# Prefix steps of a recurrent-block kernel: output projections begun on three channel blocks ahead of the last gate, the other jobs and PSUM banks dealt anew

## The chip, the cores and the metric

One core of a Trainium2 chip. The metric is device time in microseconds. Before the change: 9424.98 us, the median of 3 runs (9423.15 to 9425.7).

## The reference

Two blocks in a row, all in float32. The first is a stack of L = 4 selective state-space layers (width D = 256, inner width DI = 512, DS = 16 states a channel) over a sequence that is a 64-token context prefix followed by 512 tokens, for 16 sequences:

```
p = silu(ctx @ pre_w1) @ pre_w2;  h = concat([p, x], time)
for each layer:
    xn = rmsnorm(h) * norm_w
    xi, z = split(xn @ in_proj)
    xi = silu(causal_conv4(xi) + conv_b)
    dt, Bm, Cm = split(xi @ x_proj);  dt = softplus(dt @ dt_proj + dt_b)
    state[e, s] = exp(dt * A[e, s]) * state[e, s] + dt * Bm[s] * xi[e]      # over time
    y = sum_s state[e, s] * Cm[s] + xi * D_param
    h = h + (y * silu(z)) @ out_proj
h = rmsnorm(h)[:, 64:]
```

The second is a cross-attention and feed-forward block on h and the context.

## The kernel before

**Phases.** Since all is causal, the 64 prefix tokens of all 16 sequences are done first, for all four layers: 8 sequences of 64 tokens side by side fill 512 columns. This gives 8 *prefix steps* (4 layers x 2 halves, class `Phase` with the `PRE_` tables), and their end states are written to HBM (`kept`). Then a loop over 4 blocks of 4 sequences runs 16 *main steps* each (4 layers x 4 sequences, `MAIN_` tables), and the attention part. A step holds one layer of 512 columns.

**A step.** DVE makes 64 scans (line 989), one for each of 4 channel blocks ("chunks" 0 to 3 of 128 channels) and 16 states, in 32 *units* of two. ACT makes the decays (line 727) into a ring of 8, running ahead of the scans; PE makes the scan's inputs with small matmuls (`make_input`, line 442), a *quad* of four scans at a time, into one four-bank PSUM area that isn't doubled. So the input of quad w + 1 waits for the last scan of quad w. POOL multiplies each unit's two states with the C rows (line 1231, `product`), in the prefix after copying the end states to `save` (line 1219, `keep`). PE then adds the products up in the bank `acc` (`sum_pair`, lines 454 and 459), two units behind in the prefix.

**Jobs.** While step n scans, the engines work off *jobs* of three steps: what ends step n - 1, what later chunks of n need, and what prepares n + 1. In the tables, key v is the unit at which an engine takes the job, and the pair (name, rel) says for which step: -1, 0 or 1. Each engine takes its jobs strictly in the table's order, between its own share of the scan work. The names:
- `yev` (ACT, 738) evicts a chunk of y from `acc`; `yt` (PE, 515) transposes it; `gate` (DVE, 1039) multiplies it with silu(z); `out0`, `out1` (PE, 522) are the two halves of the output projection, each four matmul parts, one a chunk; `res` (DVE, 1044) adds the residual.
- `sq` (ACT, 747), `ms` (PE, 478), `rstd` (ACT, 750 to 755) and `norm` (DVE, 999) are the norm; `xi` (PE 484, ACT 776 to 781) and `tap` (DVE, 1017) the convolution; `z` (PE 489, ACT 788) the gate's input; `silu_x`, `silu_z` (ACT, 791 to 803); `xp` (PE 495, ACT 812).
- `bT` turns B; POOL's `diag` (1240) spreads it. `dt` (PE 505, ACT 824 to 829), `ln` (834), `q`, `less`, `ndt` (DVE, 1023 to 1034) are the softplus. `dtx` (POOL, 1252) is dt * xi, `dxT` (PE 510, ACT 839) its transpose, which the inputs of that chunk's quads need; `skip` (ACT, 843) scales xi for the sum.

A name with a point, as out0.2, is one part of it. PE writes a float32 matmul as two records, so a half of the output projection has eight.

**Banks.** Jobs use three PSUM banks, `PRE_BANK` says which. A job waits until what was in its bank before is read (`bank_free`). The pending semaphore waits stand in front of the instruction, so whatever is behind it on that engine waits too. SyncE's queue loads each layer's weights, the C rows and stores the states; its order is fixed by similar waits.

Of the kernel before, what the change touches and what calls it, by code (L numbers as in the profile page):

```python
# [15 lines left out]
KI = DI // P  # L16
# [23 lines left out]
SILU = "silu_and_others"  # L40


PRE_BANK = {"dt0": 2, "dt1": 0, "dt2": 2, "dt3": 0, "dxT0": 1, "dxT1": 1, "dxT2": 2, "yt3": 1, "out0": 0, "out1": 2,
            "dxT3": 1, "ms": 1, "xi0": 0, "xi1": 2, "xi2": 1, "xi3": 0, "yt0": 2, "z0": 2, "z1": 1, "z2": 2, "z3": 0,
            "xp": 1, "yt1": 0, "bT": 1, "yt2": 1}
MAIN_BANK = {"xi0": 2, "xi1": 1, "xi2": 2, "xi3": 0, "z0": 1, "z1": 1, "z2": 1, "z3": 2, "dt3": 2, "yt3": 0, "xp": 1,
             "out0": 0, "bT": 1, "yt0": 2, "dt0": 2, "out1": 1, "dxT3": 0, "dt1": 0, "dxT0": 1, "dt2": 0, "ms": 1,
             "dxT1": 2, "yt1": 1, "yt2": 0, "dxT2": 0}
PARTS = {"ms": KD, "xi": KD, "z": KD, "xp": KI, "out": KI}


PRE_PE = {0: [("dxT1", 0)], 2: [("dxT2", 0)], 3: [("yt3", -1)], 4: [("dxT3", 0), ("out0", -1)], 5: [("out1", -1)],
# [4 lines left out]
PRE_ACT_FIRST = {2: [("yev3", -1)], 10: [("yev0", 0)], 18: [("yev1", 0)], 26: [("yev2", 0)]}  # L57
PRE_ACT = {0: [("ln3", 0)], 1: [("dxT1", 0), ("skip2", 0)], 3: [("dxT2", 0), ("skip3", 0)], 5: [("dxT3", 0)],
# [4 lines left out]
PRE_DVE = {1: [("less3", 0), ("ndt3", 0)], 3: [("gate3", -1)], 5: [("res0", -1)], 7: [("res1", -1)],  # L63
# [6 lines left out]
PRE_POOL = {0: [("dtx2", 0)], 2: [("dtx3", 0)], 28: [("dtx0", 1)], 30: [("dtx1", 1)]}  # L70


MAIN_PE = {0: [("xi3", 1)], 2: [("z0", 1)], 4: [("z1", 1)], 5: [("dt3", 0)], 6: [("z2", 1)], 7: [("yt3", -1)],
# [85 lines left out]
def program(nc, xT, ctxT, w_early, ip_x, ip_z, xp_w, dt_w, op_w, a_log, d_par, pre_w1, pre_w2, cst,  # L159
            cst_attention, avec, wq, wk, wv, wp, w1, w2, b2, kept, c_rows, out):  # L160
    ctx = ExitStack()
    with ctx:
# [69 lines left out]
        sq = view(SLOTS, KD, S)  # L232
# [78 lines left out]
        def await_read_of(eng, ph, m, name):  # L311

            eng.wait_ge(job_read[ph.bank[name]], bank_free(ph, m, name) + 1)  # L313
# [115 lines left out]
        def _(pe):  # L429
# [35 lines left out]
            def job(ph, m, full):  # L465
# [3 lines left out]
                if part:  # L469
                    parts = [parts[int(part[0])]]  # L470
# [3 lines left out]
                if name == "ms":  # L474
                    if 0 in parts:
                        pe.wait_ge(normed.sem, normed.at(ph, m, 1))
                    for k in parts:
                        i = nc.tensor.matmul(o, ones_x, xn[:, k, :], start=k == 0, stop=k == KD - 1)
                elif name[:2] == "xi":
                    if full in ("xi0", "xi0.0"):  # L480
                        pe.wait_ge(ipx_loaded, ph.layers(m) * 16)
                        await_read_of(pe, ph, m, "ms")
                    for k in parts:
                        i = nc.tensor.matmul(o, ipx[:, k, c * P:(c + 1) * P], xn[:, k, :], start=k == 0, stop=k == KD - 1)  # L484
                elif name[0] == "z":
                    if full in ("z0", "z0.0"):
                        pe.wait_ge(ipz_loaded, ph.layers(m) * 16)
                    for k in parts:
                        i = nc.tensor.matmul(o, ipz[:, k, c * P:(c + 1) * P], xn[:, k, :], start=k == 0, stop=k == KD - 1)  # L489
                elif name == "xp":  # L490
                    if 0 in parts:
                        pe.wait_ge(xpw_loaded, ph.layers(m) * 16)
                        pe.wait_ge(silu_x.sem, silu_x.at(ph, m, 1))
                    for k in parts:
                        i = nc.tensor.matmul(o[0:XP, :], xpw[:, k, :], xs[:, par, k, :], start=k == 0, stop=k == KI - 1)  # L495
                elif name == "bT":
                    await_read_of(pe, ph, m, "xp")
                    for b in range(NB):
                        i = nc.tensor.matmul(o[:, b * XP:(b + 1) * XP], xdbl[0:XP, b::NB], eye[0:XP, 0:XP],
                                             start=b == 0, stop=b == NB - 1, is_transpose=True)  # L500
                elif name[:2] == "dt":
                    if c == 0:
                        pe.wait_ge(dtw_loaded, ph.layers(m) * 16)
                        await_read_of(pe, ph, m, "xp")
                    i = nc.tensor.matmul(o, dtw[0:DR + DS + 1, c * P:(c + 1) * P], xdbl[0:DR + DS + 1, :],  # L505
                                         start=True, stop=True)
                elif name[:3] == "dxT":
                    pe.wait_ge(dtx_ready.sem, dtx_ready.at(ph, m, c + 1))
                    for b in range(NB):
                        i = nc.tensor.matmul(o[:, b * P:(b + 1) * P], dtx[:, b::NB], eye, start=b == 0, stop=b == NB - 1,  # L510
                                             is_transpose=True)
                elif name[:2] == "yt":
                    pe.wait_ge(y_out.sem, y_out.at(ph, m, c + 1))
                    for b in range(NB):
                        i = nc.tensor.matmul(o[:, b * P:(b + 1) * P], yT[:, c % 2, b * P:(b + 1) * P], eye,
                                             start=b == 0, stop=b == NB - 1, is_transpose=True)
                else:
                    if full in ("out0", "out0.0"):
                        pe.wait_ge(opw_loaded, ph.layers(m) * 16)
                        await_read_of(pe, ph, m, "yt3")  # L520
                    for k in parts:
                        i = nc.tensor.matmul(o, opw[:, k, c * P:(c + 1) * P], zs[:, m % ZS, k, :],  # L522
                                             start=k == 0, stop=k == KI - 1)
# [943 lines left out]
```

## Time and profile before

| | |
|---|---|
| median of 3 runs | 9424.98 us |
| profiled execution | 9428.24 us, span 9426.4 us |
| PE busy | 7754.2 us (82%) |
| DVE busy | 7468.0 us (79%) |
| POOL busy | 6233.6 us (66%) |
| ACT busy | 5973.5 us (63%) |
| first scan of step 0; of the first main step | 93.2; 1137.2 us |

The prefix steps are those from 93.2 to about 1040 us. Busy shares are over the whole span, of which the prefix is a ninth. The main steps repeat 64 times after it.

### The profile page before, as it was taken

To read this page: it belongs to the slowest core of one execution; us is meant where nothing else is said; L and a number is where in the kernel's file an instruction comes from. 1 tells how busy PE (TensorE), PEld (TensorE's weight loads), DVE (VectorE), ACT (ScalarE), POOL (GpSimd) and SP (SyncE) were. 2 spreads that over 40 slices of the span, in tenths; PEclk is the share of its full clock that TensorE was granted. 3 is DMA by queue.
4 is the path that set the end of the run, shared out by engine and by line. 5 is a ranking of instruction groups with operands and counts; after the bars stand their busy time and mean duration, and the time that the engine had idled before them with its cause. 6 is when DMAs were issued, how large, how long until landed. Compare 5 with 4: busy or idle time off the path is not lost.

```text
span 9426.4 us, 188716 instructions
## 1 busy us (share of the span) xinstructions
PE 7754.2 (82%) x67360; PEld 5217.9 (55%) x67360; DVE 7468.0 (79%) x7794; ACT 5973.5 (63%) x9252; POOL 6233.6 (66%) x3268
## 2 busy tenths in 40 slices
PE   7878688888878788888878788888879788888879
PEld 4555455555563455555553455555554455555554
DVE  5777599999985399999974499999974599999963
ACT  5666477777753477777753577777753577777742
POOL 4777477777771277778761387777761478777751
PEclk8888899999989899999989899999989899999989
DMA  1111111111110111111110111111100111111100
GB/s 58 47 47 42 37 41 46 55 43 43 40 37 16 45 47 54 43 40 43 53 39 3 48 56 40 43 42 56 44 34 5 59 43 40 48 53 43 40 34 10
DMA packets 133365, 390.63 MB, mean 41 GB/s; under 512 B 49580, under 2 KB 78188, under 8 KB 95552
## 3 DMA queue, kind: packets, MB, share of 16 engines
q1 hardware_dynamic: 132416, 378.25, 11.2%
q8 instruction: 562, 9.21, 0.4%
q14 instruction: 387, 3.17, 0.1%
HBM read 364.97 MB, written 13.24 MB: 40 GB/s over the span
## 4 chain that ended last, share of the span: by engine, by line
POOL 47%; issue 32%; PE 7%; POOLq 1%; ACT 1%; DVE 1%; DMA 0%; SPq 0%; DVEq 0%; ACTq 0%
POOL arena L1231 41%; PE ps L545 3%; POOL arena L1252 3%; PE ps L675 2%; POOL arena L1240 2%; POOL arena L1270 1%; POOLq L1227 0%; PE ps L489 0%; PE ps L484 0%; DMA arena<-kept 0%; PE ps L495 0%; PE ps L612 0%; PE ps L672 0%; PE ps L505 0%; POOLq L313 0%
## 5 line engine op out<-in xcount | busy, mean ns | idle before, releaser
L1231 POOL TENSOR_TENSOR arena<-arena 128x1024 f32<-128x1024 f32 x2304 | 5428.9, 2361 | 1489.9 <-DVE arena L989 1451.6
L989 DVE TENSOR_TENSOR_SCAN arena<-arena,ps 128x512 f32<-128x512 f32 x4608 | 5490.4, 1254 | 721.5 <-PE ps L442 531.2
L727 ACT ACTIVATE arena<-arena,rate 128x512 f32<-128x512 f32 (+1 forms) x4608 | 3122.2, 714 | 1104.4 <-DVE arena L989 1098.8
L459 PEld LDWEIGHTS ps<-csts,arena 128*128 128x128 f32 x18432 | 2175.9, 145 | 564.0 <-issue 452.9
L459 PE MATMUL ps<-csts,arena 128*128 128x128 f32 x18432 | 2431.5, 281 | 26.8 <-POOL arena L1231 26.8
L442 PE MATMUL ps<-arena 32*128 32x128 f32 x36864 | 1404.3, 290 | 923.3 <-DVE arena L989 911.7
L442 PEld LDWEIGHTS ps<-arena 32*128 32x128 f32 x36864 | 1176.4, 192 | 1193.2 <-DVE arena L989 1088.3
L484 PE MATMUL ps<-arena 128*128 128x512 f32 x1152 | 681.5, 725 | 253.3 <-DVE arena L999 184.6
L1252 POOL TENSOR_TENSOR arena<-arena 128x512 f32<-128x512 f32 x288 | 365.8, 1270 | 736.7 <-DVE arena L1034 722.9
L489 PE MATMUL ps<-arena 128*128 128x512 f32 x1152 | 601.8, 640 | 18.8 <-DVE arena L1034 12.5
L522 PE MATMUL ps<-arena 128*128 128x512 f32 x1152 | 556.3, 610 | 4.4 <-DVE arena L1039 4.4
L545 PE MATMUL ps<-arena 128*128 128x512 f32 (+2 forms) x1152 | 545.0, 614 | 8.6 <-ACT arena L910 8.6
L484 PEld LDWEIGHTS ps<-arena 128*128 128x128 f32 x1152 | 232.5, 222 | 500.8 <-DVE arena L999 200.8
L1017 DVE SCALAR_TENSOR_TENSOR ps<-arena,ps 128x512 f32<-128x512 f32 x576 | 429.0, 745 | 96.6 <-ACT ps L781 90.7
L1270 POOL TENSOR_TENSOR arena<-arena 128x512 f32<-128x512 f32 x128 | 133.2, 1042 | 537.8 <-DVE arena L1157 537.8
L843 ACT ACTIVATE arena<-arena,Dall 128x512 f32<-128x512 f32 x288 | 206.5, 717 | 293.4 <-POOL arena L1252 293.4
L545 PEld LDWEIGHTS ps<-arena 128*128 128x128 f32 (+1 forms) x1152 | 218.0, 202 | 309.1 <-issue 255.6
L1198 DVE TENSOR_TENSOR arena<-ps,arena 128x256 f32<-128x256 f32 x64 | 27.2, 424 | 418.6 <-PE ps L675 418.6
L505 PE MATMUL ps<-arena 33*128 33x512 f32 x576 | 339.1, 671 | 22.7 <-DVE arena L1034 22.7
L738 ACT ACTIVATE arena<-ps 128x512 f32<-128x512 f32 x288 | 170.1, 590 | 286.2 <-PE ps L459 286.2
L1240 POOL TENSOR_TENSOR arena<-csts,arena 128x512 f32<-128x512 f32 x288 | 300.9, 1046 | 76.3 <-ACT arena L819 76.3
L824 ACT ACTIVATE arena<-ps 128x512 f32<-128x512 f32 x288 | 170.0, 590 | 236.2 <-PE ps L505 236.2
(96 smaller groups left out, 7588.4 us busy)
## 6 DMA issues: line engine op xcount, KB each, us to landing
arena<-c_rows SPq DMA_DIRECT2D x288, 1024.0 KB, 4.6
arena<-ip_x SPq DMA_DIRECT2D x20, 512.0 KB, 3.7
arena<-ip_z SPq DMA_DIRECT2D x20, 512.0 KB, 3.9
arena<-op_w SPq DMA_DIRECT2D x20, 512.0 KB, 3.8
hT<-xT SPq DMA_DIRECT2D x16, 512.0 KB, 5.0
arena<-w SPq DMA_DIRECT2D x8, 1024.0 KB, 8.5
out<-arena SPq DMA_DIRECT2D x64, 128.0 KB, 1.7
arena<-xp_w SPq DMA_DIRECT2D x20, 160.0 KB, 2.4
```

What stands on the lines that cost most here:

```text
L442: i = nc.tensor.matmul(o, dtxT[rows, c, b, :], diagB[rows, quad, b, :].rearrange("p (i s) -> p i s", s=Q), start=True, stop=True)
L459: i = nc.tensor.matmul(acc[:, b * P:(b + 1) * P], hs[:, place(n, v) + s, b * P:(b + 1) * P], eye, start=False, stop=(v + 1) % CU == 0 and ...
L484: i = nc.tensor.matmul(o, ipx[:, k, c * P:(c + 1) * P], xn[:, k, :], start=k == 0, stop=k == KD - 1)
L489: i = nc.tensor.matmul(o, ipz[:, k, c * P:(c + 1) * P], xn[:, k, :], start=k == 0, stop=k == KD - 1)
L522: i = nc.tensor.matmul(o, opw[:, k, c * P:(c + 1) * P], zs[:, m % ZS, k, :], start=k == 0, stop=k == KI - 1)
L545: last = nc.tensor.matmul(o, lhs, rhs, start=i == 0, stop=i == len(parts) - 1)
L727: nc.scalar.activation(o, i, ACT.Exp, scale=rate[:, ph.layer(n), g:g + 1]).then_inc(decay.sem, 1)
L989: nc.vector.tensor_tensor_scan(hs[:, place(n, v) + g % 2, :], dA[:, g % RING, :], quad[:, g % Q::Q], init[:, n % 2, g:g + 1] if ph.main() ...
L1017: i = nc.vector.scalar_tensor_tensor(o, w, taps[:, c, k:k + 1], acc_c, ALU.mult, ALU.add)
L1231: nc.gpsimd.tensor_tensor(hs[:, a:a + 2, :], hs[:, a:a + 2, :], Crep[:, 2 * pair:2 * pair + 2, :], ALU.mult).then_inc(prod.sem, 1)
L1240: nc.gpsimd.tensor_tensor(diagB[:, quad, :, :].rearrange("p b (i s) -> p b i s", s=Q), minus32.unsqueeze(1).unsqueeze(3).broadcast_to(shap ...
L1252: nc.gpsimd.tensor_tensor(dtx, dt[:, c, :], xs[:, m % 2, c, :], ALU.mult).then_inc(dtx_ready.sem, 1)
```

## The change

The four `PRE_` job tables and `PRE_BANK` are rewritten; the `MAIN_` tables stay. The parts out0.0 to out0.2 and out1.0 to out1.2 are put ahead of the last gate of their step, and only out0.3 and out1.3 behind it. For this the code waits for the read of yt2 (its gate) ahead of out0.0, and for that of yt3 ahead of the last part. The norm and what follows are taken earlier, dxT0 to dxT3, dtx and skip are taken later, xp is cut into parts, and all four z use one bank.

```diff
-PRE_BANK = {"dt0": 2, "dt1": 0, "dt2": 2, "dt3": 0, "dxT0": 1, "dxT1": 1, "dxT2": 2, "yt3": 1, "out0": 0, "out1": 2,
-            "dxT3": 1, "ms": 1, "xi0": 0, "xi1": 2, "xi2": 1, "xi3": 0, "yt0": 2, "z0": 2, "z1": 1, "z2": 2, "z3": 0,
-            "xp": 1, "yt1": 0, "bT": 1, "yt2": 1}
+PRE_BANK = {"out0": 1, "out1": 2, "yt3": 0, "dxT1": 0, "ms": 2, "dxT2": 0, "xi0": 1, "xi1": 2, "dxT3": 0, "xi2": 1, "xi3": 2,
+            "z0": 0, "z1": 0, "z2": 0, "z3": 0, "yt0": 1, "xp": 2, "yt1": 1, "bT": 0, "dt0": 2, "dt1": 0, "dt2": 1, "yt2": 2,
+            "dxT0": 2, "dt3": 0}
...
-PRE_PE = {0: [("dxT1", 0)], 2: [("dxT2", 0)], 3: [("yt3", -1)], 4: [("dxT3", 0), ("out0", -1)], 5: [("out1", -1)],
-          8: [("ms", 1)], 12: [("xi0", 1), ("xi1", 1)], 13: [("xi2", 1)], 15: [("xi3", 1)], 16: [("yt0", 0)],
-          18: [("z0", 1), ("z1", 1)], 20: [("z2", 1), ("z3", 1)], 21: [("xp", 1)], 22: [("yt1", 0)],
-          24: [("bT", 1), ("dt0", 1)], 26: [("dt1", 1)], 27: [("yt2", 0)], 28: [("dt2", 1)], 29: [("dxT0", 1)],
-          30: [("dt3", 1)]}
+PRE_PE = {0: [("out0.0", -1), ("out0.1", -1)], 1: [("out0.2", -1)], 2: [("out1.0", -1), ("out1.1", -1)],
+          3: [("yt3", -1), ("out1.2", -1)], 4: [("out0.3", -1), ("out1.3", -1)], 5: [("dxT1", 0)], 7: [("ms", 1)],
+          9: [("dxT2", 0)], 10: [("xi0", 1)], 11: [("xi1", 1)], 13: [("dxT3", 0), ("xi2", 1)], 14: [("xi3", 1)],
+          15: [("z0", 1)], 16: [("z1", 1)], 17: [("yt0", 0), ("z2", 1)], 18: [("z3", 1)], 20: [("xp.0", 1), ("xp.1", 1)],
+          21: [("xp.2", 1), ("xp.3", 1)], 22: [("yt1", 0)], 23: [("bT", 1), ("dt0", 1)], 25: [("dt1", 1)], 27: [("dt2", 1)],
+          28: [("yt2", 0)], 30: [("dxT0", 1), ("dt3", 1)]}
...
-PRE_ACT = {0: [("ln3", 0)], 1: [("dxT1", 0), ("skip2", 0)], 3: [("dxT2", 0), ("skip3", 0)], 5: [("dxT3", 0)],
-           7: [("sq", 1)], 9: [("rstd", 1)], 12: [("xi0", 1)], 13: [("xi1", 1)], 14: [("xi2", 1)], 16: [("xi3", 1)],
-           19: [("z0", 1), ("z1", 1)], 20: [("silu_x", 1), ("z2", 1), ("z3", 1), ("silu_z", 1)], 23: [("xp", 1)],
-           25: [("bT", 1), ("dt0", 1)], 26: [("ln0", 1)], 27: [("dt1", 1)], 28: [("ln1", 1)],
-           29: [("dt2", 1), ("skip0", 1)], 30: [("dxT0", 1), ("ln2", 1)], 31: [("dt3", 1), ("skip1", 1)]}
-PRE_DVE = {1: [("less3", 0), ("ndt3", 0)], 3: [("gate3", -1)], 5: [("res0", -1)], 7: [("res1", -1)],
-           11: [("norm0", 1), ("norm1", 1)], 13: [("tap00", 1), ("tap01", 1), ("tap02", 1)],
-           15: [("tap10", 1), ("tap11", 1), ("tap12", 1)],
-           17: [("tap20", 1), ("gate0", 0), ("tap21", 1), ("tap22", 1)],
-           19: [("tap30", 1), ("tap31", 1), ("tap32", 1)], 23: [("gate1", 0)], 25: [("q0", 1)],
-           27: [("less0", 1), ("q1", 1), ("ndt0", 1)], 29: [("less1", 1), ("gate2", 0), ("q2", 1), ("ndt1", 1)],
-           31: [("less2", 1), ("q3", 1), ("ndt2", 1)]}
-PRE_POOL = {0: [("dtx2", 0)], 2: [("dtx3", 0)], 28: [("dtx0", 1)], 30: [("dtx1", 1)]}
+PRE_ACT = {0: [("ln3", 0)], 2: [("skip1", 0)], 5: [("sq", 1)], 6: [("dxT1", 0)], 7: [("rstd", 1), ("skip2", 0)],
+           10: [("dxT2", 0), ("xi0", 1)], 12: [("xi1", 1)], 13: [("dxT3", 0), ("xi2", 1)], 14: [("skip3", 0)],
+           15: [("xi3", 1), ("z0", 1)], 16: [("z1", 1)], 17: [("z2", 1)],
+           18: [("z3", 1), ("silu_x", 1), ("silu_z", 1)], 22: [("xp", 1)], 24: [("bT", 1), ("dt0", 1)], 25: [("ln0", 1)],
+           26: [("dt1", 1)], 27: [("ln1", 1)], 28: [("dt2", 1), ("skip0", 1)], 30: [("ln2", 1)], 31: [("dxT0", 1), ("dt3", 1)]}
+PRE_DVE = {1: [("less3", 0), ("ndt3", 0)], 3: [("gate3", -1)], 5: [("res0", -1), ("res1", -1)],
+           9: [("norm0", 1), ("norm1", 1)], 11: [("tap00", 1), ("tap01", 1), ("tap02", 1)],
+           13: [("tap10", 1), ("tap11", 1), ("tap12", 1)], 15: [("tap20", 1), ("tap21", 1), ("tap22", 1)],
+           17: [("tap30", 1), ("tap31", 1), ("tap32", 1)], 19: [("gate0", 0)], 23: [("gate1", 0)], 25: [("q0", 1)],
+           27: [("less0", 1), ("ndt0", 1), ("q1", 1)], 29: [("less1", 1), ("ndt1", 1), ("gate2", 0), ("q2", 1)],
+           31: [("less2", 1), ("ndt2", 1), ("q3", 1)]}
+PRE_POOL = {6: [("dtx2", 0)], 10: [("dtx3", 0)], 28: [("dtx0", 1)], 31: [("dtx1", 1)]}
...
@@ def job
                     if full in ("out0", "out0.0"):
                         pe.wait_ge(opw_loaded, ph.layers(m) * 16)
+                        await_read_of(pe, ph, m, "yt2")
+                    if c == 0 and KI - 1 in parts:
                         await_read_of(pe, ph, m, "yt3")
```

## Rows read from the trace of the kernel before

**Rows 1.** The page: span and instructions.

```profile
span 9426.4 us, 188716 instructions
...
```

**Rows 2.** Line 747, once a step, prefix and main: durations, first and last start.

```profile
...
L747 ACT ACTIVATE arena<-hT x6: 1056/1057/1057, 237.6 to 842.4; 128x1024 f32<-128x1024 f32 x6
...
L747 ACT ACTIVATE arena<-hT x14: 1043/1047/1054, 1206.3 to 2583.0; 128x1024 f32<-128x1024 f32 x14
...
```

**Rows 3.** Busy us of each engine, PE clock, DMA: six prefix steps, thirteen main.

```profile
...
207.40:932.90 725.50, 585.19 (x5328) 418.39 (x5328) 559.04 (x578) 463.24 (x714) 540.44 (x433) 0.88 0.14 45
1245.00:2640.00 1395.00, 1170.38 (x11702) 820.90 (x11706) 1279.25 (x1267) 1009.79 (x1567) 1107.42 (x527) 0.97 0.13 46
...
```

**Rows 4.** DVE's waits in six prefix steps: us in total, times, longest.

```profile
...
DVE arena L989 <- issue: 114.8, 39, 5.7
DVE arena L989 <- PE ps L442: 41.7, 26, 5.7
...
```

**Rows 5.** DVE's timeline, one prefix step: start, us, what, idle before.

```profile
...
474.84 4.55 DVE L989 TENSOR_TENSOR_SCAN arena<-arena,ps 128x512 f32<-128x512 f32 x4 [5.68 <-PE ps L442]
...
533.08 4.55 DVE L989 TENSOR_TENSOR_SCAN arena<-arena,ps 128x512 f32<-128x512 f32 x4 [5.36 <-issue]
...
563.60 4.55 DVE L989 TENSOR_TENSOR_SCAN arena<-arena,ps 128x512 f32<-128x512 f32 x4 [3.67 <-issue]
...
569.84 2.33 DVE L989 TENSOR_TENSOR_SCAN arena<-arena,ps 128x512 f32<-128x512 f32 x2
```

**Rows 6.** PE's timeline in the same step, ahead of the fourth quad and ms.

```profile
...
464.27 0.72 PE L510 MATMUL ps<-csts,arena 128*128 128x128 f32 x4 [1.50 <-POOL arena L1252]
464.83 3.60 PE L522 MATMUL ps<-arena 128*128 128x512 f32 x8
468.27 1.04 PE L459 MATMUL ps<-csts,arena 128*128 128x128 f32 x8
...
473.55 1.17 PE L442 MATMUL ps<-arena 32*128 32x128 f32 x32
...
481.27 3.22 PE L478 MATMUL ps<-arena,csts 128*128 128x512 f32 x4 [0.39 <-ACT arena L747]
...
```

**Rows 7.** PE's timeline later in that step, ahead of quads 11 and 15.

```profile
...
522.98 3.70 PE L489 MATMUL ps<-arena 128*128 128x512 f32 x8
...
527.39 3.60 PE L495 MATMUL ps<-arena 128*80 128x512 f32 x8
...
559.56 1.10 PE L510 MATMUL ps<-csts,arena 128*128 128x128 f32 x4 [4.27 <-POOL arena L1252]
...
```

**Rows 8.** Groups in six prefix steps: busy us, mean ns, idle before and releaser.

```profile
...
L1231 POOL TENSOR_TENSOR arena<-arena 128x1024 f32<-128x1024 f32 x192 | 452.8, 2358 | 28.7 <-POOL arena L1219 4.5
...
L1219 POOL COPY arena<-arena 128x16 f32<-128x16 f32 x192 | 40.9, 213 | 156.3 <-DVE arena L989 156.3
...
L1240 POOL TENSOR_TENSOR arena<-csts,arena 128x512 f32<-128x512 f32 x25 | 26.2, 1047 | 0.0
L510 PE MATMUL ps<-csts,arena 128*128 128x128 f32 x96 | 21.9, 367 | 42.0 <-POOL arena L1252 42.0
...
```

**Rows 9.** ACT's timeline in that step: skip2, then skip0 and what follows.

```profile
...
457.58 0.72 ACT L843 ACTIVATE arena<-arena,Dall 128x512 f32<-128x512 f32 x1 [3.43 <-POOL arena L1252]
...
559.45 0.72 ACT L843 ACTIVATE arena<-arena,Dall 128x512 f32<-128x512 f32 x1 [1.50 <-POOL arena L1252]
560.08 1.31 ACT L727 ACTIVATE arena<-arena,rate 128x504 f32<-128x504 f32 x2
...
```

**Rows 10.** Timelines: ACT before step 0; PE and DVE behind step 7.

```profile
...
67.24 1.28 ACT L791 ACT_TABLE_LOAD   x1
...
74.75 0.68 ACT L812 ACTIVATE arena<-ps,csts 80x512 f32<-80x512 f32 x1
...
1046.62 9.00 PE L522 MATMUL ps<-arena 128*128 128x512 f32 x16 [0.94 <-DVE arena L1039]
1055.65 0.69 DVE L1044 TENSOR_TENSOR hT<-ps,hT 128x512 f32<-128x512 f32 x1 [2.74 <-PE ps L522]
```

## The prediction

> **What bounds the kernel now.** Read first the page: one core, span 9426.4 us [rows 1]. The tables that change steer the eight prefix steps alone, so the next view is one instruction that occurs once a step, the square of the norm. Its first and last start give a prefix step of (842.4 - 237.6) / 5 = 120.96 us, and a main step of (2583.0 - 1206.3) / 13 = 105.9 us [rows 2]. Both do the same 64 scans; the prefix alone has 32 small state copies on POOL. That is 15 us a step to ask about.
>
> The scans on DVE are the spine. Of 725.5 us (six steps) DVE is busy 559, POOL 540, PE 585, at a mean granted clock of 0.88, where the main steps have 0.97 [rows 3]. None is full, so what counts is how they wait for each other. DVE's waits are before scans: 156 us in six steps, 26 a step, 41.7 put down to the matmuls of line 442 and 114.8 to "issue", which I read as the same wait, since every long one stands at a scan that opens a group of four [rows 4]. The input of four scans (a quad) has only one buffer: line 442 for the next quad runs after the fourth scan, so each quad costs 4.55 us of scans and then 1.2 to 1.5 us, or the DVE jobs put there if they are longer, or the time until PE is through with what its order puts first.
>
> In the step from 449.88 three waits stand out: 5.68 at 474.84 (quad 3), 5.36 at 533.08 (quad 11) and 3.67 at 563.60 (quad 15) [rows 5]. PE's timeline says why. Before quad 3: the transpose dxT3, held 1.50 for POOL; then out0 3.60, sum 1.04, out1, as long, and a sum, and only then the input at 473.55, though DVE had been idle since 469.2 (474.84 - 5.68) [rows 5, 6]. Before quad 11: z2 and z3 3.70, sum, xp 3.60, sum [rows 7]. Before quad 15: dxT0, held 4.27 for POOL [rows 7].
>
> **The change, part by part.** I walk one step with durations of these rows, t counted from its first scan. On PE: a pair sum 1.0 (1.5 with its seed), input 1.2, an output part 3.60 / 4 = 0.9, xi and z 3.70 / 2 = 1.9, an xp part 0.9, dxT 0.7 [rows 6, 7], dt 1.0 (two matmuls like z's); on DVE a quad 4.55 and a job 0.7 [rows 5, 10]; on POOL a unit 2.36 + 0.21 + 0.1 = 2.7, a dtx 1.27 and a diag 1.05 [rows 8].
>
> *Units 0 to 5 (quads 0 to 3).* dtx2 and dtx3 leave POOL's units 0 and 2, and dtx1 goes behind the last product: sum31 becomes free at about 2.8 instead of 3.7, and the eviction yev3, which stood behind skip2 and its 3.43 us wait for dtx2 [rows 9], comes at 4.9 instead of 8.9. Six of the eight output parts (5.4 us) now run before the last gate. They are no fewer: until input 2, PE has out1's three parts 2.7, yt3 0.7, sums 2.5, from 5.8 to 11.7, so quad 2 still starts at 13.0, as before. Then it has only out0.3 and out1.3 (1.8 in place of 7.2), two sums 2.0 and dxT1 0.7: 12.8 + 4.5 = 17.3, under the scans' end at 17.6. Input 3 ends at 18.8, quad 3 starts at 19.0 instead of 25.0. **Gain 6.0.** The extra wait (yt2's read) is for a gate of the step before, long done; its cost is nothing. In the main table out0 and yt3 share a bank, whose own wait demands yt3's read anyway: nothing changes there.
>
> *Units 6 to 19.* Both residuals end at 18.9, the square at 20.0, ms (3.22 at the slow clock [rows 6], and a start 0.4 late) at 23.7; sum5 1.0 and input 4 1.2 follow, quad 4 starts at 26.0 (31.1 before). The two norms cover input 5 and end at 31.9. xi0 and xi1 3.8 and two sums 2.5 hold input 6 to 38.3, quad 6 starts at 39.5. The taps are two units earlier, one chunk in each of quads 6 to 9. xi3 stands on PE until tap12's read at 46.3, then 1.9, z0 1.9, two sums 2.0, input 8 at 52.1. z1, yt0, z2 and two sums, 6.5, put input 9 at 59.8. All four z use bank 0, so each waits for the eviction of the one before; by my walk these are done 1.1 to 1.6 us ahead (z1's eviction 55.8, z2's turn 56.9). Quad 10 starts at 66.9 instead of 73.3. The lead is 4 to 6.4: **no further gain** beyond 0.4.
>
> *Units 20 to 23.* z3 is done before input 10, silu_x ends at 66.7 (load 1.28 + 1.91 after z3's eviction). Between inputs 10 and 11 PE has xp's four parts 3.6 and two sums: 72.4, against the scans' end at 71.4; quad 11 starts at 73.7 instead of 83.2. **Gain 3.1.** bT and dt0 come ahead of input 12, which then starts at 79.0 (the scans end at 78.3): quad 12 at 80.3, before 89.5.
>
> *Units 24 to 31.* dxT0 leaves the place before input 15 for the place after it, so POOL's dtx0 (at 99.7) no longer holds it: quad 15 starts at once behind its DVE jobs, at 100.2 (113.7 before). What is late next is ACT: skip0 waits for dtx0 and ends at 100.4; behind it stand six decays 4.0, ln2 0.6, dxT0's eviction 0.6 and dt3's first two activations 1.3 [rows 9], to 107.0, then q3 on DVE 0.7: the next step's first scan is at 107.8, 12.2 under this step's 119.96. **Gain 2.7.** POOL carries 32 x 2.7 + 4 x 2.32 = 95 us and ends its last product 2.0 behind that scan, as I assumed at the start.
>
> So the walk gives a step of 107.8. Where nothing but scans, covered inputs and DVE jobs count, the floor is 16 x 4.55 + 29.2 = 102.0 (16 gaps of 1.5 each, or the jobs where longer).
>
> The walk has PE at full clock. Six of its intervals hang on PE: about 30 us of matmuls. At the prefix's clock of 0.88 these take 30 / 0.88 - 30 = 4.1 us more, at the main steps' 0.97 0.9 more [rows 3]. I take 2.2 (a clock near 0.93, since PE idles less): **a step of 110.0.** Against the mean of 120.96 that is 10.96 (the step walked is 1.0 shorter than the mean; I take it that what lengthens the others, PE's clock, goes with it).
>
> A row shows what idling costs: dxT takes 1.10 after 4.27 us of idling and 0.72 elsewhere [rows 6, 7], the half and the full level of TensorE's clock. The Trainium skill ("TensorE: Matmul & The Clock Gate", "A second HAM failure mode: psum-queue depth-cycling") speaks against this change: a PE that pauses briefly between groups of matmuls while cycling through PSUM banks falls back to the half clock again and again. Four z in one bank are such pauses. By that rule the clock would stay at 0.88 or fall; this is the first rival.
>
> **Ends of the run.** Step 0 has no output jobs: it gains only the second and third parts, 6. The last step has no jobs for a next one: of its wait at quad 3, as long as in the step walked [rows 5], 4.5 comes back. Behind it out0 and out1 take 9.00 us at half clock between the gate and the last residual, which ends at 1056.3 [rows 10]; four matmuls of 16 remain, 3.4, plus one part that overlaps the gate: a gain of 4.2. The other way goes the start: without scans to hide it, silu_x now stands behind z2, z3 and their bank waits instead of behind z1, at 67.24 [rows 10]: z3's eviction would end at 72.6, so xp is evicted at 80.1 rather than 75.4: a loss of 4.7. SP's queue loads weights and C rows long ahead (POOL's product 6 at 20 needs a load issued at about 3, of 5 us), so I cost its shifts at nothing; if a load came 2 us late, POOL has 13 us in hand.
>
> Sum against the profiled execution, 9428.24 us (span 9426.4): 6 x 10.96 + 6 + 4.5 + 4.2 - 4.7 = 75.8. The median of the three runs is 9424.98, 3.3 below; I give the same difference on it: **9349 us**, 0.8% faster. The main steps and the attention don't change.
>
> **The rivals.**
> 1. *The gain is eaten by the slow clock and bank waits.* A clock of 0.80 in the PE-bound intervals costs 7.5 us, a step is 115.3, the whole 9425 - 6 x 5.7 - 10 = 9381. For it: 0.88 today, the z's in one bank. Against: fewer idle stretches of PE.
> 2. *The prefix becomes as good as the main steps*, 105.9, since the same kind of order reaches that there [rows 2]: 9425 - 6 x 15.1 - 10 = 9324. Against: POOL's 32 copies, and my walk's intervals on PE.
> 3. *Slower.* PE is a queue in order: z1, z2, z3 and xp each stand for an ACT event which itself stands behind two decays, which wait for scans, which wait for PE's next input. If each of the four stands 4.4 us (two scans 2.3, decay and eviction 1.3, handing over 0.8), a step is 107.8 + 17.6 = 125.4: 9425 + 7 x 4.4 (step 0 too) - 10 = 9446. It decides from 3.3 us each (13.2 in all). Against: in the walk ACT is ahead in units 15 to 18, by 1 us in the worst case.
> 4. *No change:* the output parts are not on the path, and what is freed at quad 3 is lost again at input 4, which now waits for ms: about 9425 - 10. Against: ms costs 3.2, the freed time is 6.
>
> **How the numbers follow.** The forecast (a step of 108.5 to 112, 9336 to 9361) gets 0.54, rival 1 with all up to 118 a step 0.20, rival 2 with all under 108.5 0.18, rival 3 0.04, rival 4 0.04. Range 9327 to 9386: it takes in most of 1 and 2. A measurement here tells about 0.2% (19 us) from no change: faster 0.92, same 0.04, slower 0.04.
>
> **What would show it.** The wait at quad 3 falls from 5.7 to about 1.3, at quad 11 to about 2.3, at quad 15 to under 0.5; the one at quad 4 grows to 2.4. The squares are 110 us apart; the granted clock in the prefix rises above 0.88; dxT no longer idles PE (42 us in six steps today [rows 8]). Wrong would be: new waits of z or xi3 on PE over 2 us, decays later than their scans in units 18 to 22 (behind silu_z), or a main step other than 105.9.

## The result, and the profile after

| | median, us | ratio to the kernel before (95% interval) |
|---|---|---|
| before | 9424.98 | |
| changed, measured with the prediction | 9329.63 | 0.9891 (0.9874 to 0.9909) |
| changed, again (`after_again`) | 9321.44 | 0.9888 (0.9873 to 0.9903) |

The kernel is 1.1% faster, by 103 to 106 us of 9425 where 76 were forecast. All executions of the changed kernel but one lie between 9314 and 9330; the one left out had its TensorE clock at 0.42 on average and lifts the first median. By the two ratios the time is 9319 to 9322 us, 5 to 8 us below the range that was given (9327 to 9386).

The profile read here is that of `after_again` (span 9324.6 us). The change puts two lines ahead of the job code, so line 747 of before is 749, 989 is 991, 522 is 524. First the squares of the norm: durations, first and last start. The mean step is (760.7 - 224.5) / 5 = 107.2 us, against 120.96 [rows 2].

```profile
...
L749 ACT ACTIVATE arena<-hT x6: 1057/1058/1060, 224.5 to 760.7; 128x1024 f32<-128x1024 f32 x6
...
```

Then the windows, steps 1 to 6 and some main steps; the columns are those of [rows 3]. The six steps take 645.3 us instead of 725.5. DVE and POOL have the same work as before; PE's busy time is shorter because the clock is at 0.91 instead of 0.88.

```profile
...
206.10:851.40 645.30, 569.44 (x5329) 402.96 (x5328) 561.48 (x578) 457.41 (x717) 541.76 (x435) 0.91 0.15 50
1145.00:2535.00 1390.00, 1165.56 (x11661) 818.15 (x11659) 1274.47 (x1262) 1006.74 (x1562) 1102.41 (x525) 0.97 0.13 46
...
```

DVE's waits before scans in these steps were 156.5 us [rows 4]. Now they are less than half, 74.2 us:

```profile
...
DVE arena L991 <- issue: 48.3, 45, 2.1
DVE arena L991 <- PE ps L442: 25.9, 18, 2.0
...
```

DVE's timeline in step 3, from 421.06, answers to [rows 5]. Quad 3 opens at 439.54 after 0.25 us (the two residuals now stand in the gap before it), quad 11 at 494.54 after 2.00, quad 15 at 520.88 without a wait. The next step opens at 527.36.

```profile
...
421.06 4.55 DVE L991 TENSOR_TENSOR_SCAN arena<-arena,ps 128x512 f32<-128x512 f32 x4 [0.85 <-PE ps L442]
...
438.02 1.26 DVE L1046 TENSOR_TENSOR hT<-ps,hT 128x512 f32<-128x512 f32 x2
439.54 4.55 DVE L991 TENSOR_TENSOR_SCAN arena<-arena,ps 128x512 f32<-128x512 f32 x4 [0.25 <-issue]
445.52 4.55 DVE L991 TENSOR_TENSOR_SCAN arena<-arena,ps 128x512 f32<-128x512 f32 x4 [1.43 <-issue]
...
475.17 4.55 DVE L991 TENSOR_TENSOR_SCAN arena<-arena,ps 128x512 f32<-128x512 f32 x4 [1.74 <-PE ps L442]
...
494.54 4.55 DVE L991 TENSOR_TENSOR_SCAN arena<-arena,ps 128x512 f32<-128x512 f32 x4 [2.00 <-PE ps L442]
...
520.88 4.54 DVE L991 TENSOR_TENSOR_SCAN arena<-arena,ps 128x512 f32<-128x512 f32 x4
...
527.36 1.21 DVE L991 TENSOR_TENSOR_SCAN arena<-arena,ps 128x512 f32<-128x512 f32 x1
```

PE's timeline answers to [rows 6, 7]: behind the last gate stand four records of the output projection (1.98 us) instead of sixteen, PE is done at 437.6 and waits 0.68 for the scans' end. The norm's ms takes 1.96 us here. Ahead of quad 15 the input at 518.44 comes first, dxT and dt behind it.

```profile
...
433.36 1.98 PE L524 MATMUL ps<-arena 128*128 128x512 f32 x4
435.18 1.04 PE L459 MATMUL ps<-csts,arena 128*128 128x128 f32 x8
436.05 0.65 PE L510 MATMUL ps<-csts,arena 128*128 128x128 f32 x4
436.54 1.04 PE L459 MATMUL ps<-csts,arena 128*128 128x128 f32 x8
438.25 1.17 PE L442 MATMUL ps<-arena 32*128 32x128 f32 x32 [0.68 <-DVE arena L991]
...
440.58 1.96 PE L478 MATMUL ps<-arena,csts 128*128 128x512 f32 x4
...
```

```profile
...
518.44 2.03 PE L442 MATMUL ps<-arena 32*128 32x128 f32 x32 [1.12 <-DVE arena L991]
520.42 1.13 PE L510 MATMUL ps<-csts,arena 128*128 128x128 f32 x4
...
```

Mean waits of DVE ahead of the quads of steps 1 to 6, added up from its timelines, us; the wait of a job on DVE counts with the quad behind it:

| quad | 0 | 1, 2 | 3 | 4 to 6 | 7 | 8 to 10 | 11 | 12, 13 | 14 | 15 | all |
|---|---|---|---|---|---|---|---|---|---|---|---|
| before | 0.0 | 2.7 | 6.0 | 3.2 | 1.8 | 0.7 | 5.3 | 3.9 | 0.0 | 4.2 | 27.7 |
| changed | 0.5 | 1.5 | 0.3 | 3.8 | 0.1 | 2.2 | 2.1 | 2.4 | 1.0 | 0.1 | 13.9 |

13.1 of the 13.8 us are at quads 3, 11 and 15; what the other quads gain and lose nearly cancels. The main steps are untouched: from the first main scan (1137.2 before, 1035.3 now) to the end it is 8289.2 and 8289.3 us.

### The profile page after: what moved, and what is told of

Read it like the earlier page. It is cut to its first block, busy times and chain, and to the rows that moved or that the text cites. A ratio compares the mean times of both kernels' runs of the same rounds, so it can differ in the third digit from the quotient of the medians.

```text
span 17956.0 us, 188716 instructions
## 1 busy us (share of the span) xinstructions
PE 17614.1 (98%) x67360; PEld 9504.9 (53%) x67360; DVE 7500.5 (42%) x7794; ACT 6053.0 (34%) x9252; POOL 6224.8 (35%) x3268
## 4 chain that ended last, share of the span: by engine, by line
PE 63%; issue 22%; POOL 14%; ACT 1%; POOLq 0%; DMA 0%; DVE 0%; SPq 0%; DVEq 0%; ACTq 0%
PE ps L459 18%; POOL arena L1233 12%; PE ps L442 10%; PE ps L484 5%; PE ps L489 5%; PE ps L547 5%; PE ps L524 4%; PE ps L677 3%; PE ps L495 3%; PE ps L505 2%; PE ps L478 1%; PE ps L510 1%; PE ps L454 1%; PE ps L614 1%; PE ps L515 1%
## 5 line engine op out<-in xcount | busy, mean ns | idle before, releaser
L459 PE MATMUL ps<-csts,arena 128*128 128x128 f32 x18432 | 5746.5, 524 | 0.8 <-POOL arena L1233 0.7
L459 PEld LDWEIGHTS ps<-csts,arena 128*128 128x128 f32 x18432 | 3838.6, 217 | 2926.7 <-issue 1791.4
L442 PE MATMUL ps<-arena 32*128 32x128 f32 x36864 | 2983.6, 498 | 54.3 <-DVE arena L991 52.0
L442 PEld LDWEIGHTS ps<-arena 32*128 32x128 f32 x36864 | 2624.9, 400 | 675.3 <-issue 584.0
L484 PE MATMUL ps<-arena 128*128 128x512 f32 x1152 | 1434.7, 1432 | 55.2 <-DVE arena L1001 54.2
L489 PE MATMUL ps<-arena 128*128 128x512 f32 x1152 | 1436.4, 1418 | 15.4 <-DVE arena L1036 7.9
L524 PE MATMUL ps<-arena 128*128 128x512 f32 x1152 | 1385.6, 1383 | 3.1 <-DVE arena L1041 3.1
L547 PE MATMUL ps<-arena 128*128 128x512 f32 (+2 forms) x1152 | 1078.5, 1119 | 8.6 <-ACT arena L912 8.6
L1254 POOL TENSOR_TENSOR arena<-arena 128x512 f32<-128x512 f32 x288 | 365.7, 1270 | 1456.4 <-DVE arena L1036 1430.9
L495 PE MATMUL ps<-arena 128*80 128x512 f32 x576 | 724.5, 1421 | 8.0 <-ACT arena L790 4.0
L505 PE MATMUL ps<-arena 33*128 33x512 f32 x576 | 730.1, 1389 | 0.0
L484 PEld LDWEIGHTS ps<-arena 128*128 128x128 f32 x1152 | 364.1, 339 | 609.8 <-issue 520.7
L524 PEld LDWEIGHTS ps<-arena 128*128 128x128 f32 x1152 | 357.1, 330 | 481.4 <-issue 460.4
L489 PEld LDWEIGHTS ps<-arena 128*128 128x128 f32 x1152 | 353.3, 332 | 477.4 <-issue 412.8
```

The source lines that it names most:

```text
L442: i = nc.tensor.matmul(o, dtxT[rows, c, b, :], diagB[rows, quad, b, :].rearrange("p (i s) -> p i s", s=Q), start=True, stop=True)
L459: i = nc.tensor.matmul(acc[:, b * P:(b + 1) * P], hs[:, place(n, v) + s, b * P:(b + 1) * P], eye, start=False, stop=(v + 1) % CU == 0 and ...
L547: last = nc.tensor.matmul(o, lhs, rhs, start=i == 0, stop=i == len(parts) - 1)
```

## The experiments

All ratios are to the kernel before, with 95% intervals; `changed` stands for 0.9888 (0.9873 to 0.9903).

### after_again, after_third: the changed kernel unaltered

> The changed kernel unaltered, for an undisturbed profile. Theory S (the split of the output projection, and PE's shorter queue ahead of quads 3, 11 and 15, give the gain; the step was walked at 110.0 and is in truth nearer to 107): about 9322, steps of 106 to 108, the wait at quad 3 near 1.3, at quad 11 under 2.3, at quad 15 under 0.5, clock in the prefix above 0.93. Theory E (the steps are near the walked 110 and the missing 26 us come from the ends of the run or from the main steps): steps of 109 to 111 and the first main scan over 15 us earlier than the steps explain.

Measured: 9321.44. Theory S holds for the mean step, 107.5, though steps of about 106 and of about 109 take turns, and for the waits (0.3 at quad 3, where it had 1.3; 2.1; 0.1). Its clock does not hold: 0.91, not above 0.93. The first main scan is 101.9 us earlier, of which the six steps explain 80.2, so theory E's second half is right too: the ends gave more than thought.

> The changed kernel once more, for one more profile: its times fall into two groups, 9314 to 9316 and 9326 to 9330. Theory P (where the stretches of half clock fall within a step differs from execution to execution; in the profiled one, 9326, every second step was 109.0 instead of 106.3): a profile of the lower group has no or hardly any steps of 109, one of the upper group repeats the pattern. Rival E (the groups differ at the ends of the prefix or in the main steps): the prefix steps are the same in both.

Measured: 9329.92, one execution, again of the upper group. Its steps 1, 2 and 3 in windows (the eighth number from the left, behind the pairs of busy time and count, is the clock):

```profile
...
208.30:312.10 103.80, 90.28 (x889) 63.98 (x889) 93.50 (x96) 74.45 (x117) 88.49 (x71) 0.97 0.13 45
312.10:421.10 109.00, 96.74 (x889) 68.50 (x888) 93.61 (x97) 77.02 (x122) 91.02 (x75) 0.89 0.18 60
421.10:527.40 106.30, 93.45 (x889) 65.89 (x890) 93.42 (x96) 75.28 (x118) 89.44 (x71) 0.94 0.12 43
...
```

The same code takes 103.8 us at 0.97, 106.3 at 0.94 and 109.0 at 0.89, with DVE's busy time equal. Where the clock is low, PE's records are longer and the next quad opens later: xi3's matmuls take 3.40 us in step 2 and 1.98 in step 1, and the wait at quad 8 is 1.74 and 0.05. Steps 2 to 6 are those of `after_again` to 0.1 us; steps 0 and 1 are not (107.0 and 103.8 against 104.8 and 106.0), and the 3.5 us between the two executions lie behind the last step. No execution of the lower group was profiled with this kernel, so theory P is half shown: the upper group repeats its pattern, and a difference of 2.7 us in each of some five steps would be the 13 us between the groups.

### no_split: the split undone in the new order

```diff
-PRE_PE = {0: [("out0.0", -1), ("out0.1", -1)], 1: [("out0.2", -1)], 2: [("out1.0", -1), ("out1.1", -1)],
-          3: [("yt3", -1), ("out1.2", -1)], 4: [("out0.3", -1), ("out1.3", -1)], ...
+PRE_PE = {3: [("yt3", -1)], 4: [("out0", -1), ("out1", -1)], ...
```

> The changed kernel with out0 and out1 whole, behind the last gate at unit 4, all else as changed. Theory S: out0 and out1 (7.2 us) stand again ahead of input 3, which ends at about 22.9 instead of 18.8 after the step's first scan; 4.0 a step, lost for good: 4 x 7 = 28, some 9350. Rival R (the reorder of POOL's and ACT's jobs is what counts, and the time lost at quad 3 is caught up at the quads bound by DVE): under 8 us more than the changed kernel, 9322 to 9330.

Measured: 9352.77, 0.9928 (0.9915 to 0.9942), 31 us more than the changed kernel. PE's and DVE's timelines in its step 3 (first scan at 421.5) show the sixteen records and the wait at quad 3, which opens at 23.3 us instead of 18.5. Rival R falls. Theory S is right on the wait and on the total, but not on where the time goes: it had 4 us lost for good in each step, and in the profiled execution the steps 1 to 6 are 2.0 us longer each, while 16.7 us of the difference lie in the last step and behind it (see the table at the end of this section). And the split is the smaller part of the change: without it the kernel is still 72 us faster than before.

```profile
...
434.20 7.13 PE L523 MATMUL ps<-arena 128*128 128x512 f32 x16
...
443.49 1.17 PE L441 MATMUL ps<-arena 32*128 32x128 f32 x32
...
```

```profile
...
444.79 2.33 DVE L990 TENSOR_TENSOR_SCAN arena<-arena,ps 128x512 f32<-128x512 f32 x2 [2.73 <-PE ps L441]
```

### only_split and split_late: the split alone, in the old order

```diff
 # only_split, and the two waits of the change
-PRE_PE = {0: [("dxT1", 0)], 2: [("dxT2", 0)], 3: [("yt3", -1)], 4: [("dxT3", 0), ("out0", -1)], 5: [("out1", -1)],
+PRE_PE = {0: [("dxT1", 0)], 1: [("out0.0", -1), ("out0.1", -1), ("out0.2", -1)], 2: [("dxT2", 0)],
+          3: [("out1.0", -1), ("out1.1", -1), ("out1.2", -1), ("yt3", -1)],
+          4: [("dxT3", 0), ("out0.3", -1), ("out1.3", -1)],
 # split_late
+PRE_PE = {0: [("dxT1", 0)], 2: [("out0.0", -1), ("out0.1", -1), ("dxT2", 0)], 3: [("yt3", -1), ("out0.2", -1)],
+          4: [("dxT3", 0), ("out0.3", -1), ("out1.0", -1), ("out1.1", -1)], 5: [("out1.2", -1), ("out1.3", -1)],
```

> The kernel before with the split alone: out0.0 to out0.2 at unit 1, out1.0 to out1.2 at unit 3, out0.3 and out1.3 at unit 4; banks and the other tables as before. Theory S: input 3 ends at about 20 instead of 24.8, the wait at quad 3 falls by 4.5, kept to the end of the step: 4.5 x 7 = 31, some 9393. Rival R: the later waits (quads 11 and 15, on xp and on dxT0) take it back, under 8 us faster: 9417 to 9425.

Measured: 9437.62, 1.0013 (1.0004 to 1.0022): slower than before, and both theories missed it. PE and DVE in its step 3 (first scan at 452.5) say why. With the old banks out0 shares bank 0 with dt3, whose last reader is ndt3 on DVE behind scan 3. PE stands 2.94 us for it with input 1 queued behind, the three parts then take 4.54 us (in the changed kernel 1.98 and 1.02), and quad 1 waits 6.69:

```profile
...
458.51 4.54 PE L526 MATMUL ps<-arena 128*128 128x512 f32 x6 [2.94 <-DVE arena L1038]
...
463.86 1.17 PE L444 MATMUL ps<-arena 32*128 32x128 f32 x32
...
```

```profile
...
465.15 4.55 DVE L993 TENSOR_TENSOR_SCAN arena<-arena,ps 128x512 f32<-128x512 f32 x4 [6.69 <-ACT arena L731]
...
480.13 2.33 DVE L993 TENSOR_TENSOR_SCAN arena<-arena,ps 128x512 f32<-128x512 f32 x2 [0.85 <-issue]
```

The wait at quad 3 did fall to 0.85, as theory S had it, from 5.68; the 4.8 us were there and 6.5 were paid at quad 1.

> The kernel before with the output projection cut, as in only_split, but its parts begun behind input 1 (out0.0, out0.1 at unit 2, out0.2 at 3, the rest at 4 and 5), so that out0's bank, last used by dt3, has been read by then. Theory B (only_split lost because out0.0 stood 2.9 us for ndt3 in front of input 1, 6.7 at quad 1, while the split itself gains 4.9 at quad 3): the wait at quad 1 is back at 0.2 to 1, quad 3 starts 2 us earlier than before the change, some 9410. Rival W (ahead of the gate there is no room on PE: each part only delays the inputs of quads 1 and 2 by its own 0.9): no faster than 9425.

Measured: 9408.48, 0.9985 (0.9976 to 0.9994), theory B to 2 us. So the split is worth 15 us in the old order and 31 in the new. To begin at unit 0 it needs a bank that is free by then; the new deal of banks provides one. How much of the 16 us between the two is the banks and how much the rest of the order was not measured.

### dxT0_early and late_z: two more moves undone

```diff
 # dxT0_early: PE, ACT, POOL
-          28: [("yt2", 0)], 30: [("dxT0", 1), ("dt3", 1)]}
+          28: [("yt2", 0)], 29: [("dxT0", 1)], 30: [("dt3", 1)]}
-... 30: [("ln2", 1)], 31: [("dxT0", 1), ("dt3", 1)]}
+... 30: [("dxT0", 1), ("ln2", 1)], 31: [("dt3", 1)]}
-PRE_POOL = {... 31: [("dtx1", 1)]}
+PRE_POOL = {... 30: [("dtx1", 1)]}
```

> The changed kernel with dxT0 back in its old place (PE unit 29, ACT unit 30) and dtx1 in POOL's unit 30. Theory S: PE stands for POOL's dtx0 ahead of input 15 again, quad 15 starts 2.5 to 4 us later: 18 to 28 us more than the changed kernel, 9340 to 9350. Rival R (ACT, behind skip0, sets the end of the step anyway): under 8 us more.

Measured: 9340.3, 0.991 (0.9895 to 0.9925), 19 us more. In its step 3 (first scan at 426.6, the next step's at 535.9) PE idles 5.25 us ahead of dxT0 and quad 15 waits 4.04. Theory S holds by the total and the wait. The row names a second holder beside POOL's dtx0 (done at 524.55): gate2 on DVE (L1041, done at 524.76), which reads yt2, and yt2 has dxT0's bank in the new deal.

```profile
...
524.82 1.13 PE L510 MATMUL ps<-csts,arena 128*128 128x128 f32 x4 [5.25 <-DVE arena L1041]
...
```

```profile
...
529.41 3.44 DVE L991 TENSOR_TENSOR_SCAN arena<-arena,ps 128x512 f32<-128x512 f32 x3 [4.04 <-issue]
```

```diff
 # late_z: banks, PE and ACT
-            "z0": 0, "z1": 0, "z2": 0, "z3": 0, "yt0": 1, ...
+            "z0": 0, "z1": 2, "z2": 0, "z3": 2, "yt0": 1, ...
-          15: [("z0", 1)], 16: [("z1", 1)], 17: [("yt0", 0), ("z2", 1)], 18: [("z3", 1)], 20: [("xp.0", 1), ("xp.1", 1)],
-          21: [("xp.2", 1), ("xp.3", 1)], ...
+          17: [("yt0", 0)], 18: [("z0", 1), ("z1", 1)], 20: [("z2", 1), ("z3", 1)],
+          21: [("xp", 1)], ...
-           15: [("xi3", 1), ("z0", 1)], 16: [("z1", 1)], 17: [("z2", 1)],
-           18: [("z3", 1), ("silu_x", 1), ("silu_z", 1)], ...
+           15: [("xi3", 1)],
+           19: [("z0", 1), ("z1", 1)], 20: [("silu_x", 1), ("z2", 1), ("z3", 1), ("silu_z", 1)], ...
```

> The changed kernel with z0 to z3, silu_x, silu_z and xp back at the old units on PE and ACT (z at 18 and 20, xp whole at 21; z1 and z3 in bank 2, since z0 and z1 are taken together again), all else as changed. Theory S (the queue of PE ahead of input 11 is what the move of z and xp shortens): the wait at quad 11 grows from 2.0 back to about 5.4, the intervals of quads 8 to 10 become shorter by up to 2: net 2 to 3.5 a step, 9336 to 9346. Rival R (the total of PE's work between quads 7 and 12 is the same wherever it stands, so the place of z does not matter): within 6 us of the changed kernel.

Measured: 9333.52, 0.9907 (0.9892 to 0.9922), 12 us more, 2.5 below theory S's range, and outside rival R's 6, with intervals that overlap. The wait at quad 11 is back at 5.46. What it is worth is not shown: in the profiled execution steps 1 to 6 are 107.8 us long against 107.5, so that, as rival R had it, the time lost at quad 11 is nearly made up at the quads around it. The run also puts the z's in two banks, and its clock there is 0.95 against 0.91.

```profile
...
496.30 4.56 DVE L991 TENSOR_TENSOR_SCAN arena<-arena,ps 128x512 f32<-128x512 f32 x4 [5.46 <-issue]
```

### z_banks, dt_twice, zb_dt: PE's clock and the z's bank

```diff
 # z_banks
-            "z0": 0, "z1": 0, "z2": 0, "z3": 0, "yt0": 1, ...
+            "z0": 0, "z1": 1, "z2": 0, "z3": 2, "yt0": 1, ...
 # dt_twice
-                    i = nc.tensor.matmul(o, dtw[...], xdbl[...], start=True, stop=True)
+                    for _ in range(1 if ph.main() or c == 0 else 2):
+                        i = nc.tensor.matmul(o, dtw[...], xdbl[...], start=True, stop=True)
```

> The changed kernel with z1 in bank 1 and z3 in bank 2 instead of all four in bank 0. Theory S (each eviction is done before the next z's turn; one bank costs nothing in the steps, only about 2 us ahead of the first step, where no scans lie between): within 3 us of the changed kernel. Rival 1 of the prediction (PE pauses at each z and falls to the half clock): 10 us faster or more.

Measured: 9310.0, 0.9881 (0.9866 to 0.9896), 11 us faster than the changed kernel by the medians, which is what rival 1 asked for, with intervals that overlap. Its mechanism does not show: in steps 1 to 6 of the changed kernel (`after_again`) PE has no wait ahead of any z, just as theory S said. What differs is the clock, 0.96 in these steps against 0.91, and why it does stays open. In its profile steps 2 to 4 are 105.3, 103.6 and 103.1 us long:

```profile
...
312.40:417.70 105.30, 91.42 (x889) 64.36 (x888) 93.63 (x97) 76.98 (x122) 90.94 (x75) 0.95 0.20 63
417.70:521.30 103.60, 90.32 (x889) 63.98 (x890) 93.47 (x97) 75.14 (x119) 89.31 (x71) 0.97 0.14 45
521.30:624.40 103.10, 88.75 (x889) 62.66 (x888) 93.51 (x98) 75.95 (x121) 90.06 (x73) 0.98 0.19 63
...
```

> The changed kernel with the matmuls of dt1, dt2 and dt3 of the prefix issued twice each into the same place, 3 x 1 us more of PE's work a step, where PE idles 1.6, 0.7 and 1.1 us ahead of inputs 13, 14 and 15 today. Theory C (the steps of 109.0 against 106.3 come from half-clock stretches that follow these idle times; work in their place keeps the clock up): steps all near 106.3, 6 to 10 us faster than the changed kernel. Rival W (the added work delays inputs 13 to 15 and the sums): 5 to 15 us slower.

Measured: 9321.67, 0.9892 (0.9877 to 0.9908): the same as the changed kernel, so by the total both theories miss. The profiled steps 2 to 6 came as theory C had them, steady at 105.8 us and a clock of 0.95, and the spread is narrow (9318 to 9323). That the added 3 us of matmuls cost what the steadier clock gives is a reading, not shown by itself.

> z_banks with dt_twice. Theory C (PE's idle places ahead of inputs 13 to 15 bring half-clock stretches): steps steadily near 103 and a narrower spread than z_banks (9302 to 9319), some 9302. Rival W: the added 3 us of matmuls cost as much as they give, as dt_twice showed: 9307 to 9313.

Measured: 9321.93, 0.9888 (0.9872 to 0.9905), steps of 106.3 to 107.6, 12 us slower than `z_banks`. Theory C falls, since work put into these idle places does not bring the steps to 103, and rival W's 9307 to 9313 is missed too.

### first_old, zb_first: ahead of the first step

A second set of the four tables, the old ones without skip1, is used for n = -1 of the prefix:

```diff
+            if n == -1 and not ph.main():
+                table = FIRST.get(id(table), table)
             return [(n + rel, name) for name, rel in table.get(key, []) if ph.has(n, rel)]
```

> The changed kernel with the old order of jobs (not the old banks) in the stretch ahead of the first prefix step alone, where nothing is scanned. Theory S (the 8.1 us that the first scan comes later than before the change are silu_x and xp behind all four z, and xi2's wait for its bank): the first scan at about 96 instead of 101.3, some 5 us faster in all, which is under what the totals can tell; the profile shows it. Rival B (the banks alone make it late): first scan at 100 or later.

Measured: 9315.26, 0.9886 (0.987 to 0.9903). The first scan is at 94.4 instead of 101.3. ACT's timelines of the changed kernel and of this one show the cause: silu_x's table load at 75.24 behind all four z, or at 67.28 behind two of them. Theory S holds, but not all of the 6.9 us is the order: `no_split`, whose jobs ahead of step 0 are those of the changed kernel, has its first scan at 97.1, with ms at 1.96 us instead of 3.75 and xp at 3.63 instead of 5.15, so some 4 us of it can be the clock.

```profile
...
69.28 0.60 ACT L790 ACTIVATE arena<-ps 128x512 f32<-128x512 f32 x1 [2.07 <-PE ps L489]
...
74.63 0.60 ACT L790 ACTIVATE arena<-ps 128x512 f32<-128x512 f32 x1 [2.07 <-PE ps L489]
75.24 1.28 ACT L793 ACT_TABLE_LOAD   x1
...
83.78 0.68 ACT L814 ACTIVATE arena<-ps,csts 80x512 f32<-80x512 f32 x1 [2.23 <-PE ps L495]
```

```profile
...
66.66 0.60 ACT L815 ACTIVATE arena<-ps 128x512 f32<-128x512 f32 x1 [2.07 <-PE ps L514]
67.28 1.28 ACT L818 ACT_TABLE_LOAD   x1
...
76.97 0.68 ACT L839 ACTIVATE arena<-ps,csts 80x512 f32<-80x512 f32 x1
```

> z_banks and first_old together. If both add up: first scan at 93 to 96 and steps of 103 to 106 as in z_banks, some 9305. Rival: the steps fall into another pattern of half-clock stretches, and the total is within 5 us of the changed kernel's 9321.

Measured: 9306.29, 0.9876 (0.986 to 0.9893): first scan at 94.5, steps of 103.1 to 106.6. It beats both kernels by the median, the changed one by 15 us (0.16%), which overlapping intervals don't make certain.

### The profiled executions side by side

Each line is one profiled execution against that of `after_again`, in us. "Behind" is from the last prefix scan to the first main scan.

| | first scan | step 0 | steps 1 to 6 | last step | behind | sum | clock, steps 1 to 6 |
|---|---|---|---|---|---|---|---|
| `no_split` | -4.2 | +2.1 | +11.8 | +4.7 | +12.0 | +26.3 | 0.93 |
| `dxT0_early` | -0.5 | +2.5 | +10.2 | +1.5 | +3.3 | +16.9 | 0.92 |
| `late_z` | -4.3 | +3.8 | +1.7 | -0.2 | +2.6 | +3.5 | 0.95 |
| `first_old` | -6.9 | +0.9 | -10.2 | +0.9 | +2.9 | -12.4 | 0.93 |
| `z_banks` | -2.7 | +3.1 | -19.9 | -0.6 | +0.3 | -19.8 | 0.96 |

`first_old` changes nothing in these steps and still has six of them in 10.2 us less, so a difference of this size between single executions need not come from an edit; the clock is 0.93 there against 0.91. Undoing the split opens quad 3 4.2 us later on average; against `after_again` 2.0 us a step of that are left at the step's end, against `first_old` 3.7. For dxT0 it is 1.7 and 3.4 a step. The gains at single waits are therefore bounded here, not measured, and part of a gain at one quad can be lost again by the end of the step.

## Why the prediction was wrong

The direction was right, and so was the mechanism at the three waits; the time fell 5 us or more under the range, because two terms of the sum were too small: the step, and the ends of the run. By its steps:

- **Units 0 to 5, "Gain 6.0".** Right as an opening: quad 2 opened at 12.5 (13.0 walked), quad 3 at 18.5 (19.0). `no_split` opens it at 22.7 on average, where the kernel before had 25.0, so some 2 us of the 6 come from the other moves.
- **The rest of the walk.** Quads 4, 6, 10, 11, 12 and 15 were put at 26.0, 39.5, 66.9, 73.7, 80.3 and 100.2, and opened at 24.5, 38.9, 66.9, 73.5, 79.5 and 99.8; the next step at 106.3, not 107.8. This is a step at a clock of 0.94, while the walk has full clock; in the step at 0.97 (step 1 of `after_third`) they opened at 24.5, 37.5, 63.9, 70.7, 77.7 and 97.1, and the next step at 103.8. `dxT0_early` and `late_z` bring back the waits at quads 15 and 11, but not the walk's gains of 2.7 and 3.1 as such. The claim of cause that missed is quad 4: ms took 2.0, not 3.22, and no longer held input 4.
- **"The walk has PE at full clock ... I take 2.2".** This is the step that failed: a step of 110.0 against 107.55 on average (645.3 / 6). It gave a gain of 10.96 a step where 13.4 were measured (80.2 / 6), 14.4 us too little in six. The walk was taken as exact at full clock and then lengthened. It had already been too long: I charged ms at half clock (3.22, measured 1.96) and PE whole records, while in the rows above a sum of 1.04 begins at 435.18 and the next record at 436.05, 0.87 later, and in [rows 6] out0 of 3.60 begins at 464.83 and the sum behind it 3.44 later. At a clock of 0.97 the step is 103.8, not 107.8; which share of the 4.0 us each of the two has was not measured. The clock's price in turn was too small: between the steps at 0.97 and at 0.89 lie 5.2 us, not the 3.2 that the walk's 30 us of matmuls give between 0.97 and 0.88.
- **Ends of the run, "6 + 4.5 + 4.2 - 4.7" = 10.0.** This failed too. They gave 21.7: step 0 9.4 (114.2 to 104.8), the last step 8.5 (105.7 to 97.2 up to its last scan), what lies between it and the first main scan 11.9 (98.6 to 86.7), the start -8.1 (93.2 to 101.3). For the last step I took the wait at quad 3 alone, and less than the 5.2 that it gave; those at quads 1, 7, 8, 12 and 13 shrank by 0.5 to 0.9 each, and the last gate's own by 0.9, while those at quads 9 to 11 grew by 0.3 to 0.9. Of the 11.9 behind it, put at 4.2, 7.7 lie before the last residual's end and 4.2 between that and the first main scan, where no job of the change stands; the cause of these 4.2 is open. The start lost more than 4.7, since z3's eviction ended at 75.2, not 72.6, and xp's parts took 5.1 us (78.6 to 83.7), not 3.6. 14.4 + 11.7 are the 26 us that the forecast lacked.
- **Rival 1.** The clock in the prefix rose only to 0.91, and with the z's in three banks the time was 11 us shorter, not certain, and the clock 0.96 (`z_banks`), where rival 1 wanted 32 us. The Trainium skill ("TensorE: Matmul & The Clock Gate", "A second HAM failure mode: psum-queue depth-cycling") says that a PE which idles briefly between groups of matmuls while it cycles through PSUM banks goes back and forth between the two levels of its clock. The trace does not bear this out for the z's: PE has no wait ahead of them in steps 1 to 6, and the run that cycles through more banks has the higher clock.
- **Rival 2.** Its 9324 is nearest to the time, by luck: its step (105.9) was 1.6 too short and its ends (10) were 11.7 too small, and the two nearly cancel.
- **Rivals 3 and 4.** No z stood on PE in a step, and xi3 stood 1.05 us, for a tap on DVE. What came near to rival 4 is `only_split`, the split in the old banks and order; there the time was lost at quad 1, not at input 4.
- **The signs.** The waits at quads 3, 11 and 15 fell below what was said, the one at quad 4 grew only to 1.4, not 2.4, and dxT holds PE for 3.4 us in six steps where it was 42.

What stays open is how the gain of a step divides among the moves, and what sets the pattern of half-clock stretches, and with it the two groups of times 13 us apart.

## What to carry to other kernels

Work that is cut so that most of it runs ahead of a late input only helps if its PSUM bank is free when it begins: the last reader of that bank, on whichever engine, becomes a wait at the head of an in-order queue, and the same cut turned from 31 us of gain into 13 us of loss. A wait that returns when one move is undone shows the cause of the wait; what it is worth has to be read at the end of the step, and against more than one execution where the clock changes its pattern. When a schedule is walked, use the distance from one record's start to the next, not the record's length, and keep the clock's share apart, since rows at one clock carry it already. A gain in a repeated step has to be worked out for the first and last step and for the stretches around them by themselves; here these gave a fifth of it (21.7 of 101.9 us).

## What the runs showed of the hardware

With the same instructions and the same DVE time a prefix step took 103.8, 106.3 or 109.0 us as the granted clock of TensorE was 0.97, 0.94 or 0.89, and the lengths of steps 2 to 6 repeated from one execution to another (`after_again`, `after_third`) to 0.1 us, though steps 0 and 1 differed by 2. Giving PE 3 us more matmuls a step (`dt_twice`) left the total where it was and the steps even, at a clock of 0.95. The profiled execution of `z_banks` had a clock of 0.96 in six steps and that of `after_again` 0.91, with no wait of PE ahead of a z in either.
